# A two-layer kernel: the routing's sigmoid and 1/sqrt of the last stage move from ScalarE and VectorE to GpSimd

## The reference, cut to what matters

```python
    def _L1_ffn_ref(x, centroids, expert_biases, Ws_up, Ws_down, W_up, W_down):
        TOP_K = 8
        shared = jax.nn.silu(xf @ Ws_up) @ Ws_down
        aff = xf @ centroids.T
        biased = aff + expert_biases
        _, idx = jax.lax.top_k(biased, TOP_K)
        sel = jnp.take_along_axis(aff, idx, axis=1)
        w = jax.nn.sigmoid(sel)
        w = w / (jnp.sum(w, axis=-1, keepdims=True) + 1e-08)
        cw = jnp.zeros((T, E), dtype=x.dtype).at[jnp.arange(T)[:, None], idx].add(w)
        h = jax.nn.silu(jnp.einsum('td,edf->etf', xf, W_up))
        y = jnp.einsum('etf,efd->etd', h, W_down)
        routed = jnp.einsum('etd,te->td', y, cw)
```

## Time and profile before

| | |
|---|---|
| median of three runs | 1111.92 us (1108.44 to 1113.43) |
| span of the profiled execution | 1102.4 us; a time of its own beside the span is not given |
| median less span | 9.5 us |
| the eight tiles of the last stage | from 658.90 to the end: 443.5 us |

### The profile page before, as it was taken

The page is one execution under the profiler, slowest core; times in us unless marked ns, Lnnn a source line. Parts: engine busy times, 40 slices in busy tenths (PEclk is TensorE's granted clock), DMA queues, the critical chain, the costliest instruction groups (busy, mean ns, idle before and its releaser), DMA issues.

```text
span 1102.4 us, 20447 instructions
## 1 busy us (share of the span) xinstructions
PE 948.5 (86%) x6019; PEld 747.6 (68%) x6052; DVE 845.6 (77%) x1938; ACT 719.1 (65%) x1416; POOL 446.7 (41%) x510
## 2 busy tenths in 40 slices
PE   4652099999658999999999979999999999999998
PEld 3541099999536677677767657676767676767676
DVE  6888177777567888888888657888787878787865
ACT  4650055555346877877777657777777778787776
POOL 1378650000156665565553403333333333333333
PEclk8655599999858999999999989999999999999999
DMA  8011122222210110100100008382838383838382
GB/s 250 26 49 61 50 57 67 63 65 66 66 32 21 30 30 23 33 25 24 35 21 20 1 7 194 71 207 62 189 80 196 73 189 74 192 77 192 79 193 72
DMA packets 63921, 89.99 MB, mean 82 GB/s; under 512 B 16559, under 2 KB 54610, under 8 KB 59730
## 3 DMA queue, kind: packets, MB, share of 16 engines
q1 hardware_dynamic: 59136, 80.33, 30.4%
q0 software_dynamic: 4096, 8.40, 2.7%
q10 hardware_dynamic: 594, 0.09, 0.0%
HBM read 70.90 MB, written 17.89 MB: 81 GB/s over the span
## 4 chain that ended last, share of the span: by engine, by line
PE 63%; DVE 12%; issue 7%; ACT 7%; POOL 7%; DMA 2%; SPq 1%; DVEq 0%; POOLq 0%; ACTq 0%
POOL xs L661 6%; PE ps L2146 4%; PE ps L2128 4%; PE ps L2130 4%; PE ps L2129 4%; PE ps L2148 4%; PE ps L2147 4%; PE ps L1932 3%; PE ps L1875 3%; PE ps L1956 3%; PE ps L1950 2%; PE ps L1995 2%; PE ps L1978 2%; PE ps L1854 2%; PE ps L1853 2%
## 5 line engine op out<-in xcount | busy, mean ns | idle before, releaser
L809 POOL TENSOR_TENSOR hl<-h,hh 128x512 fp32r<-128x512 f32 x128 | 165.6, 1294 | 292.1 <-ACT hh L1081 292.1
L1081 ACT ACTIVATE hh<-h 128x512 fp32r<-128x512 f32 (+1 forms) x264 | 165.1, 625 | 44.2 <-DVE h L1711 42.7
L1711 DVE TENSOR_TENSOR h<-ps,cwB 128x512 f32<-128x512 f32 x192 | 130.5, 680 | 45.3 <-ACT ps L1070 35.5
L1611 DVE TENSOR_REDUCE nm<-ps 128x4 f32<-128x512 f32 (+1 forms) x128 | 116.4, 951 | 35.7 <-PE ps L1978 33.8
L715 POOL DMA_INDIRECT yg<-ys,gps x64 | 63.0, 985 | 166.4 <-issue 155.9
L1070 ACT ACTIVATE ps<-ps 128x512 f32<-128x512 f32 x192 | 111.7, 582 | 26.2 <-PE ps L2130 25.6
L2146 PE MATMUL ps<-hh,wh 128*128 128x512 f32 x256 | 106.1, 414 | 11.4 <-DVE hl L1718 10.4
L2128 PE MATMUL ps<-xh,wh 128*128 128x512 f32 x256 | 105.0, 410 | 0.0
L2129 PE MATMUL ps<-xl,wh 128*128 128x512 f32 x256 | 101.6, 397 | 0.0
L2130 PE MATMUL ps<-xh,wl 128*128 128x512 f32 x256 | 101.4, 396 | 0.0
L2148 PE MATMUL ps<-hh,wl 128*128 128x512 f32 x256 | 101.3, 396 | 0.0
(11 more groups left out here) (326 smaller groups left out, 2692.3 us busy)
## 6 DMA issues: line engine op xcount, KB each, us to landing
cwB<-cwd SPq DMA_DIRECT2D x32, 1536.0 KB, 14.4
cwd<-cwS SPq DMA_DIRECT2D x64, 96.0 KB
xb<-xs SPq DMA_DIRECT2D x72, 64.0 KB, 1.8
ys<-yb SPq DMA_DIRECT2D x72, 64.0 KB, 1.6
x_res<-in_L_attn_x_dram SPq DMA_DIRECT2D x4, 512.0 KB, 6.8
wst<-in_L_ffn_W_up_dram SPq DMA_DIRECT2D x32, 64.0 KB, 2.2
wst<-in_L_ffn_W_down_dram SPq DMA_DIRECT2D x32, 64.0 KB, 1.9
out_dram<-y SPq DMA_DIRECT2D x8, 256.0 KB, 13.2
```

The lines of the kernel that those rows point to most:

```text
L809: pool.tensor_tensor(hl4[:, slot(u), :], h4[:, slot(u), :], hh4[:, slot(u), :].bitcast(F32), op=ALU.subtract).then_inc(u_hlp, 1)
L1081: act.activation(hh4[r, slot(u), :], h4[r, slot(u), :], ACT.Copy).then_inc(u_hh, 1)
L1611: ins = dve.tensor_reduce(nm[:, u, 4 * g:4 * g + 4], o, axis=AX.X, op=ALU.max, negate=True)
L1711: dve.tensor_tensor(h4[:, slot(u), :], first, second, op=ALU.mult).then_inc(u_h, 1)
```

## The change

ScalarE no longer computes Exp and Ln in the tiles of the last stage. GpSimd computes both with powers: 1/sqrt as (variance + eps) to the power -0.5 behind its `hl` of unit 5, and the sigmoid in two halves of 128 x 128, behind its `hl` of units 15 and 17. Each half has three operations: e^-1 to the power of the affinity, minus (-1), and the result to the power -1. The addition and the reciprocal on VectorE fall away. VectorE's routing steps stand at other units (norm 10 to 6, high 13 to 12, and so on), and the transposition and the affinities on TensorE one unit earlier. The first tile's routing, made in the attention stage, keeps Exp on ScalarE.

```diff
+            own.done(pool.memset(inv_e[:, :], math.exp(-1.0)))
+            own.done(pool.memset(neg_half[:, :], -0.5))
+            own.done(pool.memset(neg_one[:, :], -1.0))
...
+            def x4_rstd(n, p):
+
+                pool.wait_ge(d_mv, n + 1)
+                apart(pool, pool_passed)
+                pool.tensor_scalar(lnv[:, p, :], mv[:, p, :, 1], LN_EPS, None, ALU.add).then_inc(act_d, 1)
+                pool.wait_ge(act_d, n + 1)
+                pool.tensor_tensor(rstd[:, p, :], lnv[:, p, :], neg_half[:, :].broadcast_to([P, SUB]), op=ALU.pow).then_inc(d_rs, 1)
+
+            def x4_sigmoid(n, k):
+
+                half = slice(k, k + 2)
+                made = 6 * (n - 1) + 1 + 3 * (k // 2)
+                if k == 0:
+                    pool.wait_ge(d_afc, n + 1)
+                    apart(pool, pool_passed)
+                pool.tensor_tensor(g4[:, 0, half, :], inv_e[:, :].unsqueeze(2).broadcast_to([P, 2, E2]), af[:, half, :],
+                                   op=ALU.pow).then_inc(d_ex, 1)
+                pool.wait_ge(d_ex, made + 1)
+                pool.tensor_tensor(g4[:, 2, half, :], g4[:, 0, half, :], neg_one[:, :].unsqueeze(2).broadcast_to([P, 2, E2]),
+                                   op=ALU.subtract).then_inc(d_ex, 1)
+                pool.wait_ge(d_ex, made + 2)
+                pool.tensor_tensor(g4[:, 3, half, :], g4[:, 2, half, :], neg_one[:, :].unsqueeze(2).broadcast_to([P, 2, E2]),
+                                   op=ALU.pow).then_inc(d_ex, 1)
+
             def pool_tile(t, p, before, N, S):
                 for u in range(1, NU, 2):
...
                     pool.tensor_tensor(hl4[:, slot(u), :], h4[:, slot(u), :], hh4[:, slot(u), :].bitcast(F32),
                                        op=ALU.subtract).then_inc(u_hlp, 1)
+                    if u == 5 and S:
+                        x4_rstd(t + 2, p)
+                    if u in (X4_EXP, X4_EXP + 2) and N:
+                        x4_sigmoid(t + 1, u - X4_EXP)
...
-                    if u == 12 and N:
+                    if u == X4_TURN and N:
                         x4_T(t + 1, 1 - p)
-                    if u == 16 and N:
-                        act.preload_act_table_set(TABLE)
-                        x4_exp(t + 1, 1 - p)
-                        if S:
-                            x4_rstd(t + 2, p)
...
-                    dve.wait_ge(d_ex, n + 1)
-                    own.done(dve.tensor_scalar(g4[:, 2, :, :], g4[:, 0, :, :], 1.0, None, ALU.add))
+                    if first:
+                        dve.wait_ge(d_ex, 1)
+                        own.done(dve.tensor_scalar(g4[:, 2, :, :], g4[:, 0, :, :], 1.0, None, ALU.add))
+                        own.need(own.n)
+                        own.done(dve.reciprocal(g4[:, 3, :, :], g4[:, 2, :, :]))
+                    else:
+                        dve.wait_ge(d_ex, 6 * n + 1)
...
-                        then(lambda: dve.reciprocal(g4[:, 3, :, :], g4[:, 2, :, :])),
...
-            STEP_AT = (10, 13, 14, 15, 16, 17, 18, 19, 20, 21, 22, 23, 24, 25, 26, 27, 28)
+            STEP_AT = (6, 12, 13, 14, 15, 16, 17, 18, 22, 22, 23, 24, 24, 25, 26, 27)
```

More of the change, by code:

```diff
@@ L8 @@
+import math
 from contextlib import ExitStack
@@ L90, in bass_two_layers @@
         eps_c = sb("eps_c", [P, 1], F32)
+        inv_e = sb("inv_e", [P, 1], F32)
+        neg_half = sb("neg_half", [P, 1], F32)
+        neg_one = sb("neg_one", [P, 1], F32)
         RT = 2 * SUB
@@ L439, in x4_bank @@
             return bank[3] if isinstance(n, int) and n == 0 else bank[6]
+        X4_TURN, X4_LOGITS, X4_EXP = 11, 13, 15
         def slot(u):
@@ L1489, in routing @@
             def routing(n, p):
-                own = Tickets(dve, dve_d, n * DVE_D)
+                first = isinstance(n, int) and n == 0
+                own = Tickets(dve, dve_d, 0 if first else DVE_D + (n - 1) * (DVE_D - 2))
                 def norm():
@@ L1560, in weights @@
                                       op=ALU.subtract).then_inc(d_cs, 1)
-                    assert own.n == DVE_D, own.n
+                    assert own.n == (DVE_D if first else DVE_D - 2), own.n
                 return [norm, high, low, affinity, biased, largest, replaced, chosen, sigmoid,
-                        then(lambda: dve.reciprocal(g4[:, 3, :, :], g4[:, 2, :, :])),
                         then(lambda: dve.tensor_tensor(g4[:, 4, :, :], g4[:, 3, :, :], g4[:, 1, :, :], op=ALU.mult)),
@@ L1742, in dve_tile @@
             def dve_tile(t, p, before, N, S):
-                steps = dict(zip(STEP_AT, routing(t + 1, 1 - p))) if N else {}
+                steps = list(zip(STEP_AT, routing(t + 1, 1 - p))) if N else []
                 if before is not None:
@@ L1754, in dve_tile @@
                         result(*before)
-                    if u in steps:
-                        steps[u]()
+                    for at, step in steps:
+                        if at == u:
+                            step()
             tiles_of(dve, dve_tile)
@@ L2171, in pe_tile @@
                         out_T(before[0])
-                    if u == 12 and N:
+                    if u == X4_TURN and N:
                         x4_turned(t + 1, t if before is not None else None)
-                    if u == 14 and N:
+                    if u == X4_LOGITS and N:
                         x4_logits(t + 1)
```

## The result

The changed kernel takes 1653.14 us, the median of four runs (1648.76 to 1654.13), against 1110.86 for the kernel before on the same chip: 1.4865 times as long, with an interval of 1.4827 to 1.4903. It is 542 us slower, where 19.5 us faster (1111.9 - 1092.4) was forecast.

The account below looks back on a forecast made before the run. TensorE bounds the last stage, waiting 4.49 us a tile, mostly behind ScalarE's stop. Gain 3.28 - 0.4 = 2.9 us, seven tiles 20.3, less 0.5 and 0.3: 19.5, so 1111.9 - 19.5 = 1092.4 us; range 1084 to 1108.

Parts of the forecast that it names:

- what the change adds: GpSimd, last stage: two halves per tile of power, subtraction, power, costing TensorE 0.4 us a tile; start constants 0.3 us once.
- X: GpSimd's time for one power of 128 columns: 1.1 us estimated, between bounds of 0.45 and 1.57.
- H: GpSimd's time for one half of the sigmoid, two powers, a subtraction and two hand-overs: 2.8 us, bounds 1.5 and 3.75.
- the form 2 (H - 2.6): TensorE's added wait per tile at unit 19's `hl`, from the time of a half on GpSimd: 0.4 us forecast.
- the gain of 3.28: TensorE's waits per tile in us: 1.77 over units 20 to 24, 0.53 for an `hl`, 0.98 for `cs`.
- The free 1.5 us per pair: GpSimd starts an `hl` every 2.80 us and works 1.30, leaving 1.5 us free per pair of units.
- The slack: Time between the end of GpSimd's `hl` of unit 13 and its reader on TensorE: 2.2 us.
- the power is slow: Rival: GpSimd's power at 1.8 us or more makes the kernel slower; at 3 us, 1145 us; chance 0.13.
- TensorE's need of a tile: A last-stage tile with routing would take 50.51 us without waits; 4.49 of its 55.00 us is waiting.
- the stop of ScalarE: 3.45 us per last-stage tile without a silu, two table loads and three activations; the change removes it in seven tiles.
- VectorE as the limit: Rival: VectorE waits for GpSimd's powers, gain shrinks to 1.77 + 0.4 - 0.7 = 1.4 us a tile, 1102 us; chance 0.2.
- The 9.5 us between span and median: The profiled execution's span, 1102.4 us, lay 9.5 us under the median; span forecast about 1083, median 1092.4.

Follow-up runs that it names:

- e1: The changed kernel with a multiplication in place of each power on GpSimd (output not the reference's): 1072.61 us, 0.9680 of the kernel before.
- e5: The kernel before with the new order of routing steps alone, Exp and Ln still on ScalarE, reciprocal on VectorE: 1099.35 us, 0.9919 of the kernel before.
- e13: The changed kernel with tanh for the sigmoid, its constant beside eps_c so all tiles lie as in the kernel before: 1086.34 us, 0.9772.
- e4: The changed kernel with the sigmoid as (1 + tanh(x/2)) on ScalarE, GpSimd keeping only the 1/sqrt by power: 1069.40 us, 0.9657 of the kernel before.
- e7: The changed kernel with both powers of a half on 8 columns in place of 128: 1104.43 us, 0.9966 of the kernel before.

## Why the prediction was wrong, point by point

**The step that failed** is the price of the power in "what the change adds": "Its bound above I take from the only iterative operation", VectorE's reciprocal, 1.57 us, and from it "I take X = 1.1 us". It is 20.72 us, 19 times the value taken and 13 times the bound. The reciprocal is an operation of another engine; that one engine's ratio of a hard to a plain operation (5) carries over to another was an assumption, and none of the rows supported it. On GpSimd the ratio is 0.159 to 0.0022 us a column, 72. The text said itself that nothing excludes a dearer power, and then gave that case 0.13, with 3 us as its example, and cut the range at 1108. A cost that no row prices should have carried a range in which the loss is open.

**What followed from a right price** would have been nearly right, in part by luck. With H = 42.0, the form 2 (H - 2.6) less the gain of 3.28 gives 75.5 us a tile, 529 in all; measured were 538 in the seven tiles, 542 in the medians. The free 1.5 us per pair holds. The slack was 1.3 us and not 2.2, and the lower clock behind each stop, about 4 us a tile in all, was missing; against that the gain without the powers was 5.0 us a tile (55.0 to 50.0 in e1) and not 3.28. The rival "the power is slow" is what happened, at its place (`hl` of units 17 and 19, then VectorE ahead of L1602), and its threshold of 1.8 us for a power lies between two measured kernels: the one with 1.63 us is 0.3% faster than before, the one with 2.89 us 3.6% slower. That is luck too, as both the gain and the stall behind it were put too low.

**TensorE's need of a tile**, 50.51 us, was right: with tanh and the tiles at their old addresses it takes 50.62. That the stop of ScalarE and what follows from it are worth this much was right too, and too small in the sum: I counted 3.28 us of the 4.49 and left the rest unassigned; the experiment gives 4.4, of which the order alone is 1.2 (e5). All of it hung on the one stop and the order.

**VectorE as the limit** did not come. In the changed kernel's long powers VectorE's operations with two SBUF inputs were hardly held up, see below; the worst case was L1602, which meets GpSimd's `hl`: 1.39 to 1.48 us in each of the seven tiles, and 1.45 to 1.47 in e1, where 0.42 is usual, and TensorE had no wait in e1's usual tile all the same. The sum of this rival has a slip: 1.77 + 0.4 - 0.7 adds the stall of 0.4 us, which would have to be taken off, and no row gives a gain of that size; it should be 0.7 us a tile, 5 us, 1107. The forecast does not rest on it.

**The price of a table load** by the Trainium skill (ScalarE: Activation LUTs, What ACT_TABLE_LOAD costs), 2.66 us for a switch: no run here shows the drain in it. The stop in e5 was 1.28 + 0.42 + 0.28 + 0.20 + 1.28 with gaps of hundredths; the 3.45 us of the earlier trace rows have no room for it either.

**The 9.5 us between span and median** were read as something around each execution. In the runs for which both are known the two differ by 1.7 to 1.8 us (1654.13 and 1652.4; 1652.31 and 1650.5): with 1.8 us more the profiled execution of before took 1104.2 us, a quick one.

## What to carry to other kernels

Before work is moved to an engine, its operation is priced on that engine by one small run, and where only the profile is at hand, an operation without a row there gets an open end, not the ratio of another engine. An engine that is 40% busy is free only in pieces: here 1.5 us per pair of units, and what is longer delays the next item of its queue and, behind its slack, everyone. If the aim is to keep one function table, look first for the same value from functions of the table that is loaded: tanh gave the sigmoid, and with the new order it took 26 us off at unchanged addresses (e13); with the tiles 32 bytes further, in another session, it was 39 us (e4). And a stop of TensorE can cost more than its length: in e7 the same stop was followed by 1.6 us of matmuls at the lower clock in some tiles and by none in others.

## What the runs showed of the hardware that was not expected

- A power on GpSimd takes 0.36 us and 0.159 us a column of 128 partitions; a subtraction of 128 columns 0.40 us.
- It does not hold VectorE up for its length. GpSimd's power ran from 832.10 to 852.83, and VectorE's two-input operations in it took their usual time but for the one that began with it (timelines of the changed kernel, GpSimd and VectorE):

```profile
832.10 20.73 POOL L829 TENSOR_TENSOR g<-inv_e,af 128x128 f32<-128x128 f32 x1
```

```profile
832.14 0.91 DVE L1755 TENSOR_TENSOR hl<-h,hh 128x512 fp32r<-128x512 f32 x1
834.36 0.41 DVE L1568 TENSOR_TENSOR g<-mr,bi 128x256 f32<-128x256 f32 x1
835.29 0.68 DVE L1755 TENSOR_TENSOR hl<-h,hh 128x512 fp32r<-128x512 f32 x1
```

  The first took 0.23 us more than the 0.68 that it has alone. Over all powers of the changed kernel the 7 `hl` that began with one took 0.82 to 0.92 us, and the 14 that began within one 0.67 to 0.68. The Trainium skill (SBUF — State Buffer, Who interferes with whom) has the pair of ports locked by whichever starts first; for GpSimd's subtraction of 1.3 us the traces agree (and L1602 above), for the power they don't, as far as its whole length goes. Why is open.
- Behind a stop TensorE's granted clock can be 0.50, and 5 to 13 matmuls then start every 0.43 us in place of 0.23. Behind the stops of 1.0 us in e7 it never was, behind those of 2.0 us in four of seven tiles, behind those of 38 to 39 us in the changed kernel always.
- A shift of all tiles behind `eps_c` by 32 bytes a partition changed the pace of the matmuls by 3% at a granted clock of 1.00 in both; a shift by 64 did not. What TensorE meets there, and which of the tiles it is, was not tried.
